# A GNN, attention and gated-cell layer on one core: the normalized input is no longer turned on TensorE, but loaded a second time already turned

## The chip, the core and the metric

The kernel runs on one core of a Trainium2 chip, as one program. The metric is the time of one execution in microseconds on the device; the median of three runs is given. Engines are named as in the profile: PE (TensorE), DVE (VectorE), ACT (ScalarE), POOL (GpSimd), SP (SyncE, which issues most transfers).

## What is computed

N = 1250 rows of D = 1024 numbers, 40000 edges of 8 types. Cut to what matters:

```
xn = layernorm(x)                                    # per row: (x - mean) / sqrt(var + eps)
u  = xn @ root + bias + sum_r mean_r(xn over edges) @ weight[r]
z  = concat(u, xn) @ w_gate + b_gate
h  = tanh(u) * z + xn * (1 - z)
q, k = elu(xn @ Wq) + 1, elu(xn @ Wk) + 1;  v = xn @ Wv;  g = sigmoid(xn @ Wg + bg)
kv = per head k.T @ v;  attention = (q * SCALE) @ kv / (q @ k_sum) * g @ Wo
x1 = x + h + attention
out = x1 + sigmoid(..) * tanh(sigmoid(..) * tanh(..))   # three products of layernorm(x1)
```

## The kernel before

**Products.** Rows are taken in T = 10 tiles of 128 (the last has 98). The work is a list of units, `UNIT`, numbered q: one stage (a weight half of 512 columns) times one tile. Stages run in the order Y (8 relation weights, two halves each), R, V, K, V, K, X, G, Q, O, C, then I, T, F twice. A unit is K = 8 steps k, and each step is three matmuls, since every operand is held as a high part (fp32r) and a low part (the rest): high by high, high by low, low by high. `aThi` and `aTlo` hold the turned activations, `Whi` and `Wlo` the weights. A unit's sums go to one of three banks of `acc` (q % 3) and leave it on ACT (Y and V, `evict`, L982) or DVE.

**How the order is set.** Each engine's instructions are written out by hand, with semaphores. All engines walk the same list of units and steps; work beside the products is hung on a unit and a step by tables. For the input x these are `LN_AT` (in which unit tile t is normalized on DVE, `ln_x`) and `TURN_AT` (in which unit tile t is turned). The first twelve units take the two halves of relation 0 tile by tile, so tile 1 is first needed in unit 2, tile 2 in unit 4, tile 3 in unit 6, tile 4 in unit 8, tile 5 in unit 10, tiles 6 to 9 in units 12 to 15.

**Input path.** For tile t: SP loads `xr` (a ring of XS = 4 tiles); DVE takes mean and variance (`bn_stats`, `bn_aggr`), ACT the root, DVE refines it in four tiny operations and writes `xnb` (L1143); PE turns it in eight 128x128 transposes into `tp` (`turn_x`, L815); ACT casts them to `aThi` (L974), DVE takes the rest into `aTlo` (L1121), and PE may start the tile (`x_lo`). POOL adds `xr` and `xnb` (`rows_sum`, L1620), and SP stores both (`x_rows`); `next_x(t)` waits until the sum of tile t is stored and loads tile t + XS into its place.

**Weights.** `hi_w` casts a granule of 128x1024 to `Whi` on ACT (L970), `lo_w` takes the rest on DVE (L1116); granules 2, 3, 5 and 7 of the first eight are done on POOL (`POOL_LO`, L1696).

**Later.** In stage K, `exponent` (ACT: relu L993, exp L995) and `elu_high` (DVE, L1399) make elu + 1 in `res`, and `kv_tile` (PE, L850) adds k.T @ v per pair of heads six steps into the next unit. In stage Q (24 units of 384 or 482 columns, `Wq` stationary, L955) the same chain ends in `read_out` (PE, L864) five steps into the next unit. The sums of R, X, G and of the last stages leave PSUM with a bias added, on DVE (L1420).

Of the kernel before, what the change touches and what calls it, by code (L numbers as in the profile page):

```python
# [14 lines left out]
N = 1250  # L15
D = 1024
# [33 lines left out]
XS = 4  # L50
# [3 lines left out]
U_SEMS, TH_SEMS = 6, 4  # L54
POOL_LO = (2, 3, 5, 7)
# [52 lines left out]
KIND = [STAGE[s][0] for s, _ in UNIT]  # L108
BY_ACT_TO = [sum(k in BY_ACT for k in KIND[:q + 1]) for q in range(UNITS)]
# [4 lines left out]
LN_AT = {0: 2, 2: 3, 4: 4, 6: 5, 7: 6, 8: 7, 9: 8, 10: 9}  # L114
TURN_AT = {1: 1, 3: 2, 5: 3, 7: 4, 8: 5, 9: 6, 10: 7, 11: 8, 12: 9}
# [81 lines left out]
def build(nc, x, src, dst, edge_type, weight, root, bias, w_gate, b_gate, Wq, Wk, Wv, Wg, bg, Wo,  # L197
          W_iT, b_i, W_oT, b_o, W_cT, b_c, out):
    with ExitStack() as ctx:
# [19 lines left out]
        code_d = dram("code_d", [RUN_ROWS, RUN])  # L219
        sample_d = dram("sample_d", [SAMPLES])  # L220
# [24 lines left out]
        stats = put("stats", [128, 16])  # L245
        x1_stats = put("x1_stats", [128, T, 12])
# [19 lines left out]
        xnb = at(M + 16384, "xnb", [128, XS, D])  # L266
        e_at = M + 32768
# [20 lines left out]
        most = at(M + 45248, "most", [128, T])
        assert M + 45312 <= end and M + 41024 + up(16 * COLS) + 32 * T <= M + 44512
# [44 lines left out]
        assert M + 49472 <= end  # L334
# [15 lines left out]
        def turned_rows(w):  # L350
# [4 lines left out]
        w_hi, w_lo, w_lo_pool, prod = sem("w_hi"), sem("w_lo"), sem("w_lo_pool"), sem("prod")  # L355
# [7 lines left out]
        ln_var, ln_root, ln_done, xs_made, x_turned, x_hi, x_lo = (  # L363
            sem(n) for n in ("ln_var", "ln_root", "ln_done", "xs_made", "x_turned", "x_hi", "x_lo"))
# [52 lines left out]
        def wait_w_lo(engine, n):  # L417

            if n in POOL_LO:
# [1384 lines left out]
```

## Time and profile before

| | before |
|---|---|
| median of 3 runs | 2206.23 us (2205.47 to 2206.28) |
| the profiled execution: time / span | 2205.51 us / 2203.7 us |
| PE busy | 2185.2 us, 99% of the span |
| DVE, ACT, POOL busy | 1176.2, 439.2, 737.6 us |
| granted PE clock, mean | 0.998 |

The span runs from the first to the last instruction; the time of the execution lies 1.8 us above it. A busy share is that of the whole span; matmuls overlap, so it says that PE had always one in flight, not that it ran at its peak.

### The profile page before, as it was taken

The numbers are of one execution on the slowest core, as the hardware profiler recorded it, in microseconds if no ns is written. First come the engines' busy times: TensorE is split into PE (matmuls) and PEld (weight loads), VectorE is DVE, ScalarE is ACT, GpSimd is POOL, SyncE is SP. The second block draws the span as 40 slices with busy tenths as digits, with TensorE's granted clock in tenths as the row PEclk, the third lists the DMA queues.
The fourth block names the chain that finished last, engine by engine and source line by source line (L and its number), as shares of the span: only waits on it lengthen the run. The fifth ranks groups of instructions, "written<-read, shape, count | busy, mean of one in ns | idle before, by whom it ended". The sixth has DMA issues, their size and how long they took to land.

```text
span 2203.7 us, 25068 instructions
## 1 busy us (share of the span) xinstructions
PE 2185.2 (99%) x9858; PEld 1776.6 (81%) x9858; DVE 1176.2 (53%) x1606; ACT 439.2 (20%) x617; POOL 737.6 (33%) x601
## 2 busy tenths in 40 slices
PE   7999999999999999999999999999999999999998
PEld 6878888888888888888888888889988888888887
DVE  5322678726666666676665676653432367234233
ACT  3221111211111111100221200112321314121121
POOL 5203002055555555544645354621210453000000
PEclk9999999999999999999999999999999999999999
DMA  7543321457788988784969788853126885103102
GB/s 251 183 131 97 109 85 48 134 183 220 261 293 281 312 301 306 242 271 141 318 223 318 238 292 299 274 177 134 49 77 225 274 285 170 39 29 125 59 30 79
DMA packets 191153, 416.59 MB, mean 189 GB/s; under 512 B 33938, under 2 KB 44563, under 8 KB 191035
## 3 DMA queue, kind: packets, MB, share of 16 engines
q1 hardware_dynamic: 127834, 229.10, 30.8%
q0 software_dynamic: 63200, 185.89, 25.4%
q8 instruction: 77, 1.26, 0.2%
q14 instruction: 42, 0.34, 0.0%
HBM read 352.34 MB, written 103.66 MB: 207 GB/s over the span
## 4 chain that ended last, share of the span: by engine, by line
PE 99%; DVE 1%; DMA 0%; ACT 0%; SPq 0%; issue 0%; DVEq 0%; ACTq 0%
PE acc L960 91%; PE acc L955 5%; PE tp L815 2%; PE agg L864 1%; PE tp L850 0%; PE misc L850 0%; DMA Wraw<-in_L_gnn_weight 0%; DVE Wlo L1116 0%; DVE stats L1135 0%; PE misc L864 0%; DVE aTlo L1519 0%; ACT L995 0%; DVE stats L1128 0%; ACT Whi L970 0%; SPq L515 0%
## 5 line engine op out<-in xcount | busy, mean ns | idle before, releaser
L960 PE MATMUL acc<-Whi,aThi 128*128 128x512 f32 (+1 forms) x2880 | 1141.2, 396 | 3.9 <-DVE aTlo L1519 2.1
L960 PE MATMUL acc<-Whi,aTlo 128*128 128x512 f32 (+1 forms) x2880 | 1135.4, 394 | 0.0
L960 PE MATMUL acc<-Wlo,aThi 128*128 128x512 f32 (+1 forms) x2880 | 1131.9, 393 | 0.0
L960 PEld LDWEIGHTS acc<-Whi,aTlo 128*128 128x128 f32 (+1 forms) x2880 | 534.1, 185 | 134.0
L960 PEld LDWEIGHTS acc<-Whi,aThi 128*128 128x128 f32 (+1 forms) x2880 | 534.2, 186 | 133.6 <-DVE aTlo L1519 2.5
L960 PEld LDWEIGHTS acc<-Wlo,aThi 128*128 128x128 f32 (+1 forms) x2880 | 535.3, 186 | 131.5
L1657 POOL DMA_INDIRECT ring<-y_d,edge x390 | 488.0, 1251 | 424.9 <-DVE U L1312 154.4
L1116 DVE TENSOR_TENSOR Wlo<-Wraw,Whi 128x1024 fp32r<-128x1024 f32 x148 | 185.5, 1255 | 314.6 <-ACT Whi L970 313.8
L982 ACT COPY res<-acc 128x512 f32<-128x512 f32 (+1 forms) x180 | 105.7, 587 | 837.7 <-PE acc L960 823.4
L1312 DVE SCALAR_TENSOR_TENSOR U<-ring,edge,U 128x1024 f32<-128x1024 f32 x180 | 230.2, 1279 | 24.2 <-DMA ring<-y_d,edge 24.0
L1312 DVE SCALAR_TENSOR_TENSOR odd<-ring,edge,odd 128x1024 f32<-128x1024 f32 x170 | 217.4, 1279 | 24.6 <-DMA ring<-y_d,edge 24.3
L970 ACT CAST Whi<-Wraw 128x1024 fp32r<-128x1024 f32 x152 | 158.9, 1047 | 199.6 <-DMA Wraw<-in_L_gnn_w_gate 71.9
L1420 DVE TENSOR_TENSOR res<-acc,bias_sb 128x512 f32<-128x512 f32 x100 | 69.2, 692 | 217.9 <-PE acc L960 128.5
L1644 POOL DMA_INDIRECT slot_d<-table,slot x20 | 21.8, 1088 | 227.9 <-DVEq L1272 222.4
L1028 ACT ACTIVATE res<-res 128x512 f32<-128x512 f32 (+1 forms) x60 | 38.0, 633 | 286.0 <-DVE res L1420 286.0
L1399 DVE SCALAR_TENSOR_TENSOR res<-acc,res 128x512 f32<-128x512 f32 (+3 forms) x44 | 28.0, 637 | 105.9 <-ACT res L995 105.9
L1121 DVE TENSOR_TENSOR aTlo<-tp,aThi 128x1024 fp32r<-128x1024 f32 (+1 forms) x39 | 46.7, 1197 | 59.9 <-ACT aThi L974 59.9
L1767 POOL TENSOR_TENSOR og<-og,part 128x384 f32<-128x384 f32 (+1 forms) x32 | 27.7, 875 | 128.2 <-DVE part L1452 128.2
L955 PE MATMUL acc<-aThi,Whi 128*128 128x384 f32 (+1 forms) x192 | 69.9, 364 | 0.0
L955 PE MATMUL acc<-aThi,Wlo 128*128 128x384 f32 (+1 forms) x192 | 67.6, 352 | 0.0
L955 PE MATMUL acc<-aTlo,Whi 128*128 128x384 f32 (+1 forms) x192 | 67.5, 352 | 0.0
L993 ACT ACTIVATE res<-acc 128x512 f32<-128x512 f32 (+3 forms) x44 | 24.4, 555 | 183.0 <-PE acc L960 94.5
(165 smaller groups left out, 1053.1 us busy)
## 6 DMA issues: line engine op xcount, KB each, us to landing
y_d<-res SPq DMA_DIRECT2D x144, 256.0 KB
Wraw<-in_L_gnn_weight SPq DMA_DIRECT2D x64, 512.0 KB, 5.6
Wraw<-in_L_gnn_w_gate SPq DMA_DIRECT2D x16, 512.0 KB, 6.7
ring<-y_d,edge POOLq DMA_INDIRECT x390, 6.3
xr<-in_x SPq DMA_DIRECT2D x9, 512.0 KB, 4.3
xn_d<-xnb SPq DMA_DIRECT2D x9, 512.0 KB, 5.4
xs_d<-xr SPq DMA_DIRECT2D x9, 512.0 KB, 5.8
ur_d<-res SPq DMA_DIRECT2D x18, 256.0 KB
```

Source lines behind the costliest of these rows:

```text
L815: tr = nc.tensor.transpose(tp[:, k // 4, (k % 4) * 128:(k % 4) * 128 + w], parts(k), ident[0:w, 0:w])
L955: mm = nc.tensor.matmul(to, a[:, s % 2, k, cols], b[:, k, c0:c0 + w], start=start, stop=stop)
L960: mm = nc.tensor.matmul(to, a[:, k, rows(i)], b[:, s % 2, k, :], start=start, stop=stop)
L970: nc.scalar.copy(granule(Whi, n), granule(Wraw, n)).then_inc(w_hi, 1)
L982: nc.scalar.copy(res[0:width(i), q % 3, :], acc[0:width(i), q % 3, :]).then_inc(evac_a, 1)
L1028: nc.scalar.activation(a, a, ACT.Tanh if kind == T_ else ACT.Sigmoid).then_inc(gate_act, 1)
L1116: nc.vector.tensor_tensor(granule(Wlo, n), granule(Wraw, n), granule(Whi, n).bitcast(F32), ALU.subtract).then_inc(w_lo, 1)
L1121: nc.vector.tensor_tensor(aTlo[:, :, rows(t)], turned_rows(width(t)), aThi[:, :, rows(t)].bitcast(F32), ALU.subtract).then_inc(done, 1)
L1312: nc.vector.scalar_tensor_tensor(to, g, scale, to, ALU.mult, ALU.add).then_inc(u_acc, 1)
L1399: nc.vector.scalar_tensor_tensor(a, p, 0.0, a, ALU.max, ALU.add).then_inc(evac_v, 1)
L1420: nc.vector.tensor_tensor(to, p, bias_sb[0:w, n % 2, :], ALU.add).then_inc(evac_v, 1)
L1657: pool.indirect_dma_start(ring[:, j % RING, :], None, a, bass.IndirectOffsetOnAxis(ap=index, axis=0), bounds_check=top - 1, oob_is_err=Fal ...
```

## The change

- **Turned input.** The host passes x a second time, turned (`x_t`). SP loads tile t of it into `xt` (`load_xt`). A DVE operation subtracts the row's mean there (`mid_x`); the mean of each row, which now runs along the free dimension, is spread over the partitions by one matmul of ones with a diagonal of means (`spread_mean`, the diagonal `mean_on` made by ACT in `root_x`). ACT casts it to `aThi` (`hi_x`), DVE takes the rest (`lo_x`). The eight transposes of each tile are gone.
- **Inverse deviation later.** What is in `aThi` and `aTlo` is only centred. `rs` holds each row's inverse deviation and its negative. It is multiplied in where sums leave PSUM: as the scale of ACT's copies (Y, V) and of the relu of K, in a `scalar_tensor_tensor` in place of the add (R, X, G), in an extra DVE operation for K, and for Q, whose rows lie along the free dimension, in an extra DVE operation `scale_q` before the relu, with `rs_row` loaded from DRAM.
- **Rings and places.** XS is 3, not 4, so x of tile 3 is no longer among the first loads. `LN_AT` and `TURN_AT` change: tile 2 is normalized in unit 1, not 0; tiles 4 to 9 are centred one unit earlier.
- **First low parts.** All eight first granules are done by `lo_w` on DVE; POOL starts its row sums when they are done.
- **kv.** `kv_tile` does one matmul per head (64 stationary columns, 65 moving), the two heads of a pair to partitions 0 to 63 and 64 to 127, instead of one per pair (128 and 130).
- **Last unit.** Its columns are done in two halves, each evicted, gated and stored by itself.

```diff
-XS = 4
+XS = 3
-POOL_LO = (2, 3, 5, 7)
-LN_AT = {0: 2, 2: 3, 4: 4, 6: 5, 7: 6, 8: 7, 9: 8, 10: 9}
-TURN_AT = {1: 1, 3: 2, 5: 3, 7: 4, 8: 5, 9: 6, 10: 7, 11: 8, 12: 9}
+LN_AT = {1: 2, 2: 3, 4: 4, 6: 5, 7: 6, 8: 7, 9: 8, 10: 9}
+TURN_AT = {1: 1, 3: 2, 5: 3, 6: 4, 7: 5, 8: 6, 9: 7, 10: 8, 11: 9}
...
             load_x(0)
-            for n in range(4):
+            load_w(0)
+            load_xt(0)
+            for n in range(1, 4):
                 load_w(n)
             load_x(1)
             load_w(4)
             load_w(5)
-            load_x(2)
+            load_xt(1)
             load_w(6)
             load_w(7)
-            load_x(3)
+            load_x(2)
+            load_xt(2)
...
                 sp.wait_ge(xs_st[t % XS], 16 * (t // XS + 1))
                 load_x(t + XS)
+                load_xt(t + XS)
...
+            def spread_mean(t):
+                pe.wait_ge(mean_root, 2 * t + 1)
+                if t:
+                    pe.wait_ge(x_mid, with_halves(t - 1))
+                w = width(t)
+                nc.tensor.matmul(tp[:, 0, 0:w], ones_all[0:w, :], mean_on[0:w, t % 2, 0:w], start=True, stop=True
+                                 ).then_inc(mean_mm, 1)
...
                 for m in range(4):
-                    to = (misc[:, :] if m < 2 else tp[:, 0, :])[:, m % 2 * 130:m % 2 * 130 + 130]
-                    mm = nc.tensor.matmul(to, rows_k[:, m * 128:(m + 1) * 128], vld[0:w, t % 2, m, :],
-                                          start=(t == 0 and m % 2 == 0), stop=(t == T - 1), skip_group_check=True)
+                    for e in range(2):
+                        head = (2 * m + e) * HEAD
+                        mm = nc.tensor.matmul(misc[e * HEAD:(e + 1) * HEAD, m * 65:m * 65 + 65], rows_k[:, head:head + HEAD],
+                                              vld[0:w, t % 2, m, e * 65:e * 65 + 65], start=(t == 0 and m == 0),
+                                              stop=(t == T - 1), skip_group_check=True)
...
+                nc.scalar.activation(mean_on[0:w, t % 2, 0:w], ident[0:w, 0:w], ACT.Copy, scale=stats[0:w, 12:13]
+                                     ).then_inc(mean_root, 1)
+                act.wait_ge(ln_stats, 2 * t + 2)
+                nc.scalar.activation(stats[0:w, 15:16], stats[0:w, 14:15], ACT.Sqrt).then_inc(mean_root, 1)
...
+            def mid_x(t, part):
+                dve.wait_ge(xt_in[t % XS], 16 * (t // XS + 1))
+                dve.wait_ge(mean_mm, t + 1)
+                a, w = xt[:, t % XS, part, 0:width(t)], width(t)
+                mean = tp[:, 0, 0:w].unsqueeze(1).to_broadcast([128, part.stop - part.start, w])
+                nc.vector.tensor_tensor(a, a, mean, ALU.subtract).then_inc(x_mid, 1)
+            def lo_x(t, part, count):
+                dve.wait_ge(x_hi, count)
+                nc.vector.tensor_tensor(aTlo[:, part, rows(t)], xt[:, t % XS, part, 0:width(t)],
+                                        aThi[:, part, rows(t)].bitcast(F32), ALU.subtract).then_inc(x_lo, 1)
...
+            def scale_q(q):
+                i, h, n = UNIT[q][1], STAGE[UNIT[q][0]][2], 3 * STAGE[UNIT[q][0]][2] + UNIT[q][1] // 4
+                w = GROUPS[i // 4][1]
+                dve.wait_ge(prod, q + 1)
+                dve.wait_ge(rs_in[n % 2], 16 * (n // 2 + 1))
+                p = acc[:, q % 3, 0:w]
+                nc.vector.tensor_tensor(p, p, rs_row[:, n % 2, 0:w], ALU.mult).then_inc(q_scaled, 1)
...
-            for n in POOL_LO:
-                pool.wait_ge(w_hi, n + 1)
-                nc.gpsimd.tensor_tensor(granule(Wlo, n), granule(Wraw, n), granule(Whi, n).bitcast(F32),
-                                        ALU.subtract).then_inc(w_lo_pool, 1)
+            pool.wait_ge(w_lo, 2 * GRAN)
             rows_sum(0)
```

**SP, after the first loads.** The names: `xn_d` and `xs_d` are the stores of tile t's normalized rows and sums, `xr<-in_x` a load of a further tile. Before, the load waits for the store of tile 0 alone and stands ahead of tile 1's two stores:

```order
L720 DMA xn_d<-xnb 128x1024 [waits ln_done]
L722 DMA xs_d<-xr 128x1024 [waits xs_made]
L519 DMA xr<-in_x 128x1024 [waits xs_st0]
L720 DMA xn_d<-xnb 128x1024 [waits ln_done]
L722 DMA xs_d<-xr 128x1024 [waits xs_made]
L552 DMA y_d<-res 128x512 [waits evac_a]
```

That load is tile 4. In the changed kernel the first such load is tile 3:

```order
L743 DMA xn_d<-xnb 128x1024 [waits ln_done]
L745 DMA xs_d<-xr 128x1024 [waits xs_made]
L743 DMA xn_d<-xnb 128x1024 [waits ln_done]
L745 DMA xs_d<-xr 128x1024 [waits xs_made]
L528 DMA xr<-in_x 128x1024 [waits xs_st0]
L533 DMA xt<-in_x_t 128x8x128 [waits x_lo]
L572 DMA y_d<-res 128x512 [waits evac_a]
```

It has moved behind the store of tile 1's sums, and so behind POOL's second row sum.

**DVE, units 2 and 3.** Before, the low part of the tile turned in unit 3 (L1121) comes between the statistics of tile 3 (`x_in3`) and those of tile 4 (`x_in0`):

```order
L1128 BN_STATS stats<-xr 128x6 [waits x_in3]
L1128 BN_STATS stats<-xr 128x6
...
L1143 TENSOR_SCALAR xnb<-xr,stats 128x1024 [waits dve_step]
L1121 TENSOR_TENSOR aTlo<-tp,aThi 128x8x128 [waits x_hi]
L1128 BN_STATS stats<-xr 128x6 [waits x_in0]
```

Changed, tile 3's statistics wait for the ring's place 0 (`x_in0`), and the centring (L1234) and low part (L1239) of tile 2 follow them:

```order
L1207 BN_STATS stats<-xr 128x6 [waits x_in0]
L1207 BN_STATS stats<-xr 128x6
...
L1225 TENSOR_SCALAR xnb<-xr,stats,rs 128x1024 [waits xs_made,xn_st0]
L1234 TENSOR_TENSOR xt<-xt,tp 128x1024 [waits mean_mm,xt_in2]
L1239 TENSOR_TENSOR aTlo<-xt,aThi 128x8x128 [waits x_hi]
```

One instruction has been added ahead of the low part, and what they stand behind waits for a later load.

**POOL, from the first row sum.** In the changed kernel:

```order
L1754 TENSOR_TENSOR xr<-xr,xnb 128x1024 [waits ln_done,w_lo]
L1832 MEMSET caps 128x1 x10
...
L1759 CAST code<-raw_edges 125x320 [waits edges_in]
...
L1846 IOTA next_places 128x128
L1754 TENSOR_TENSOR xr<-xr,xnb 128x1024 [waits ln_done] x8
```

Before it stood the same way, with four `Wlo` granules ahead of it in place of the wait for `w_lo`: the edge codes lie between the first row sum and the second in both.

## Rows read from the trace of the kernel before

**Rows 1.** The page: busy us (share of the span) x instructions.

```profile
PE 2185.2 (99%) x9858; PEld 1776.6 (81%) x9858; DVE 1176.2 (53%) x1606; ACT 439.2 (20%) x617; POOL 737.6 (33%) x601
```

**Rows 2.** Groups on PE by shape: xcount | busy us, mean ns | idle before.

```profile
L850 PE MATMUL tp<-vld,res 128*128 128x130 f32 x72 | 11.0, 274 | 0.0
```

**Rows 3.** The chain that ended last: start us, us, what.

```profile
23.16 1.71 PE tp L815 x8
...
86.31 0.87 PE tp L815 x8
92.75 0.68 PE tp L815 x8
...
1091.38 0.45 PE tp L850 x4
...
2198.10 0.70 DVE res L1420
...
2200.22 0.69 DVE res L1513
```

**Rows 4.** Timeline of the start, all engines: start us, us, engine, line [idle before].

```profile
0.74 1.28 ACT L1054 ACT_TABLE_LOAD   x1 [0.74 <-PEq L1791]
...
5.64 0.21 DVE L1130 BATCH_NORM_AGGREGATE stats<-stats 128x2 f32<-128x12 f32 x1
...
11.76 2.40 DVE L1116 TENSOR_TENSOR Wlo<-Wraw,Whi 128x1024 fp32r<-128x1024 f32 x1
...
11.90 0.79 PE L960 MATMUL acc<-Whi,aThi 128*128 128x512 f32 x1 [2.12 <-DVE aTlo L1519]
...
15.48 0.47 PE L960 MATMUL acc<-Whi,aTlo 128*128 128x512 f32 x1
...
21.23 0.50 PE L960 MATMUL acc<-Whi,aThi 128*128 128x512 f32 x1 [1.82 <-DVE Wlo L1116]
```

**Rows 5.** Timeline of POOL from 20 us.

```profile
23.38 3.37 POOL L1620 TENSOR_TENSOR xr<-xr,xnb 128x1024 f32<-128x1024 f32 x1
26.69 0.40 POOL L1700 MEMSET caps<- 128x1 f32 x10
...
35.35 7.11 POOL L1620 TENSOR_TENSOR xr<-xr,xnb 128x1024 f32<-128x1024 f32 x3
```

**Rows 6.** Line 519, the loads of x: issue to landing.

```profile
DMA to landing us min/median/max: 3.5/4.3/12.2
```

**Rows 7.** Timeline of ACT: ends of units 1, 3, 12 and 13.

```profile
29.61 0.59 ACT L982 COPY res<-acc 128x512 f32<-128x512 f32 x1 [1.84 <-PE acc L960]
...
41.66 0.59 ACT L982 COPY res<-acc 128x512 f32<-128x512 f32 x1 [3.22 <-PE acc L960]
...
97.73 0.59 ACT L982 COPY res<-acc 128x512 f32<-128x512 f32 x1 [3.45 <-PE acc L960]
103.29 0.59 ACT L982 COPY res<-acc 128x512 f32<-128x512 f32 x1 [4.97 <-PE acc L960]
```

**Rows 8.** Timeline of DVE: one tile's statistics, normalization and low part.

```profile
63.62 1.27 DVE L1128 BATCH_NORM_STATS2 stats<-xr 128x6 f32<-128x512 f32 x2
...
66.39 0.16 DVE L1134 RECIPROCAL stats<-stats 128x1 f32<-128x1 f32 x1 [1.06 <-ACT stats L1054]
...
67.22 0.81 DVE L1143 TENSOR_SCALAR xnb<-xr,stats 128x1024 f32<-128x1024 f32 x1
68.93 1.22 DVE L1121 TENSOR_TENSOR aTlo<-tp,aThi 128x1024 fp32r<-128x1024 f32 x1 [0.89 <-ACT aThi L974]
```

**Rows 9.** Timeline after the second Q unit, all engines.

```profile
1499.55 0.56 DVE L1399 SCALAR_TENSOR_TENSOR res<-acc,res 128x384 f32<-128x384 f32 x1 [1.82 <-ACT res L995]
...
1500.60 0.81 PEld L864 LDWEIGHTS agg<-kv,res 128*128 128x128 f32 x6
```

**Rows 10.** Timelines of DVE and PE after the first K unit.

```profile
1089.52 0.69 DVE L1399 SCALAR_TENSOR_TENSOR res<-acc,res 128x512 f32<-128x512 f32 x1 [6.47 <-ACT res L995]
1090.78 0.61 PE L850 MATMUL misc<-vld,res 128*128 128x130 f32 x4
```

More of the change, by code:

```diff
@@ L194, in wait, with build @@
         engine.wait_ge(self.sem, self.n)
-def build(nc, x, src, dst, edge_type, weight, root, bias, w_gate, b_gate, Wq, Wk, Wv, Wg, bg, Wo,
+def build(nc, x, x_t, src, dst, edge_type, weight, root, bias, w_gate, b_gate, Wq, Wk, Wv, Wg, bg, Wo,
           W_iT, b_i, W_oT, b_o, W_cT, b_c, out):
@@ L415, in granule @@
             return a[:, s % 2, 2 * g:2 * g + 2, :]
-        def wait_w_lo(engine, n):
-            if n in POOL_LO:
-                engine.wait_ge(w_lo_pool, POOL_LO.index(n) + 1)
-            else:
-                engine.wait_ge(w_lo, n + 1 - sum(m < n for m in POOL_LO))
         def load_beside(q):
@@ L727, in next_x, with store_rs, load_rs @@
                 load_x(t + XS)
+                load_xt(t + XS)
+            def store_rs():
+                sp.wait_ge(ln_done, T)
+                for t in range(T):
+                    sp.dma_start(rs_d[rows(t)].rearrange("(p o) -> p o", o=1), rs[0:width(t), 0, t:t + 1]
+                                 ).then_inc(rs_st, 16)
+            def load_rs(h, g):
+                n = 3 * h + g
+                c0, w = GROUPS[g]
+                if n >= 2:
+                    wait_evicted(sp, place(Q_, (n - 2) // 3, 4 * ((n - 2) % 3) + 3))
+                sp.dma_start(rs_row[:, n % 2, 0:w], rs_d[c0:c0 + w].rearrange("(o n) -> o n", o=1)
+                             .to_broadcast([128, w])).then_inc(rs_in[n % 2], 16)
             x_rows(0)
@@ L960, in _ @@
                             mm = nc.tensor.matmul(to, a[:, k, rows(i)], b[:, s % 2, k, :], start=start, stop=stop)
-                mm.then_inc(prod, 1)
+                if q != FINAL:
+                    mm.then_inc(prod, 1)
+                    continue
+                for e, c in enumerate(FINAL_PARTS):
+                    for k in range(K):
+                        for a, b, start, stop in ((aThi, Whi, k == 0, False), (aThi, Wlo, False, False),
+                                                  (aTlo, Whi, False, k == K - 1)):
+                            mm = nc.tensor.matmul(final_sums(e), a[:, k, rows(i)], b[:, s % 2, k, c], start=start,
+                                                  stop=stop)
+                    mm.then_inc(prod, 1)
         @block.scalar
@@ L981, in evict @@
                 act.wait_ge(prod, q + 1)
[L982 removed]
+                if s < 2:
+                    act.wait_ge(ln_done, i + 1)
+                nc.scalar.activation(res[0:width(i), q % 3, :], acc[0:width(i), q % 3, :], ACT.Copy,
+                                     scale=rs[0:width(i), 0, i:i + 1]).then_inc(evac_a, 1)
             def exponent(q):
@@ L1028, in gate_function, with final_gate @@
                 nc.scalar.activation(a, a, ACT.Tanh if kind == T_ else ACT.Sigmoid).then_inc(gate_act, 1)
+            def final_gate():
+                for e, c in enumerate(FINAL_PARTS):
+                    act.wait_ge(evac_v, BY_DVE_TO[FINAL] + e)
+                    a = res[0:width(T - 1), FINAL % 3, c]
+                    nc.scalar.activation(a, a, ACT.Sigmoid).then_inc(gate_act, 1)
             def cell_tanh(q):
@@ L1538, in _ @@
                             make_x1(q - 1)
+                        if kind == Q_:
+                            scale_q(q - 1)
                     if q and k == 2:
```

247 lines of the change are left out of this document (152 added, 95 removed).

## The prediction

> **What bounds the kernel now.** I read the page first: PE is busy for 99% of the span, so only what lengthens or shortens PE's own stream counts, and any other engine counts where PE waits for it [rows 1]. Then I read the groups on PE by shape and the chain that ended last, for what PE does beside the products: the transposes of x take 1.71 us once and then 0.87 us a tile (0.68 us for the last of 98 rows), nine of them inside the units, and a `kv_tile` takes 2 x 0.45 us, in eight instructions [rows 2, 3]. Then the timelines: of the start, where PE begins its first product at 11.90 us and waits 1.82 us once more, at 21.23 us, for a low part of a weight [rows 4]; of ACT, whose copies mark where units end: unit 1 at 29.61, unit 3 at 41.66, unit 12 at 97.73, unit 13 at 103.29, so that a unit with nothing beside it is 5.56 us [rows 7]. From there on PE's stream has no hole but at the first Q unit, so a change at the start passes to the end in full.
>
> **The start, up to the end of unit 1.** The statistics of tile 0 are there at 5.85 us [rows 4]. ACT now makes the diagonal first, which needs a table other than the root's, and its load stands behind the wait for the statistics; before, the only load ran at 0.74 us under the wait for x [rows 4]. That puts 1.28 us on the path: 7.1 us; the diagonal some 0.3 us, the mean's matmul at the low clock some 0.7 us: 8.2 us. Two centring halves (0.69 us each is what the halves took before, about half of the 1.22 us of [rows 8]) end near 9.7; the small operations 1.0, the normalization 0.81 [rows 8], the first weight granule and the first low half 1.8 us: PE starts near 13.6 us, 1.7 us later. DVE then has all eight granules and tile 1's statistics (some 4 us), at 1.2 us a granule, and is through at about 26.1 us. Before, POOL did four, but a DVE granule beside it took 2.40 us [rows 4]; that is given back, so unit 1 ends near 30.4 us and not 29.61. **+0.8 us**, between -1 (POOL's absence pays for more) and +3 (the third transfer, in pieces of 512 B, delays every weight behind it).
>
> **Units 2 and 3.** Two units of 5.56 and one mean matmul instead of a turn of 0.87 us. A mean is a 128-column matmul in two instructions; by the transposes, one instruction each, 0.109 us [rows 3], it is 0.22 us. **-0.65 us.** PE could begin unit 4 at 41.4 us.
>
> **The hole before unit 4.** This is the term that decides. With XS = 3, x of tile 3 is not among the first loads. By the order, SP issues it only behind the store of tile 1's sums, which waits for POOL's second `rows_sum`; between POOL's first and second stand the edge codes. POOL starts the first when the eighth low part is done, 26.1 us; a row sum undisturbed is 7.11 / 3 = 2.4 us: 28.5. From `caps` to the second sum POOL took 35.35 - 26.69 = 8.66 us [rows 5], less 0.2 for the memset that is moved ahead: 37.0; the second sum: 39.4. Store and load are issued by 39.8, and a load of x lands after 4.3 us, 3.5 at best [rows 6]: 44.1. DVE has stood in `ln_x(3)` since 34 us, and tile 2's centring and low part, which PE needs for unit 4, are queued behind it. From the landing: statistics to normalized rows took 67.22 + 0.81 - 63.62 = 4.4 us with 1.06 us of waiting for ACT [rows 8]; with ACT free, a diagonal and one more small operation it is 3.9: 48.0. Centring 1.2, ACT's cast 1.05, low part 1.2, three hops between engines: 51.6. PE waits from 41.4 to 51.6: **+10.2 us**. Bounds: 7 if POOL starts 2 us sooner and the load lands in 3.5; 13 if the sums take the 3.37 us of [rows 5] and the load 6.
>
> After it PE is cold: the first product's eight matmuls took 15.48 - 11.90 = 3.58 us at the lower level, where eight at the higher take 8 x 5.56 / 24 = 1.85 [rows 4, 7]. **+1.7 us**, 0 to 3.
>
> **Units 4 to 12.** Before, 97.73 - 41.66 = 56.07 us [rows 7]: nine units and seven turns, 6.0 us. Now seven means, 1.5 us: **-4.5 us**. But in units 6 to 10 DVE has a tile's statistics (3.9), another's centring (1.2), the wait for the cast (1.1) and the low part (1.2): 7.4 us for a PE unit of 5.78. PE's mean matmul of tile t waits for the centring of tile t - 1. In unit 8 there are 0.9 us to spare, in unit 9 it is 0.7 late, in 10 and 11 1.65 each: **+4.0 us**, 0 to 6.
>
> The new low part reads two SBUF tiles, where the old read PSUM. Beside a POOL operation such an instruction took 2.40 us instead of about 1.2 [rows 4]. POOL's sum starts with the end of the normalization and lasts 2.4 us, the low part is due 2.3 us after it: 0.1 us, in the bounds. The Trainium skill (SBUF — State Buffer, "Who interferes with whom") says so as a rule: a DVE instruction with two SBUF inputs is shut out while a GpSimd instruction that reads SBUF runs. By that rule every low part could meet a sum and wait up to 2.4 us; the row agrees on the mechanism, and the order of the two decides that little is lost.
>
> **kv.** Twenty tiles, 0.90 us each. The moving columns are the same in total (16 x 65 for 8 x 130), so at the same rate it stays 0.90. No row shows matmuls on half of the columns. If both halves ran at once, 0.45 us: -9 us. If each of 16 instructions took what the smallest on record took, 0.68 / 8 = 0.085 us [rows 3], 1.36 us: +9 us. I take near the same rate, **+1 us**. The Trainium skill (TensorEngine Tiling (Array Packing), "Key Properties") says that tiles run in parallel, which would give the -9, and that a change of tiling mode drains the engine, which pushes the other way twice a tile. No row of this trace decides between them. The extra DVE operation fits: the first K unit's single one ended at 1090.21 and kv's first matmul began at 1090.78 [rows 10], its weights being loaded some 0.3 us earlier, so 0.7 us more is 0.4 us late, once; the others have 1.8 us.
>
> **Q.** In a 384-column unit the relu waits for `scale_q`, 0.56 us and a hop, 0.6. The high part was done at 1500.11, and PE loads it as weights at 1500.60 [rows 9]: 0.46 us of cover, so 0.14 us late in each of 16 units, 2.2; 0.6 in the first, where PE waits already; 0.3 where a turned tile holds DVE. **+3.1 us**, 0 to 6.
>
> **The end.** Four operations, 2198.10 to 2200.91 [rows 3]. In halves, of the second half remain its add, then two each of multiply and add at about 0.4: 2.0 us. **-1.0 us**, with a smaller store. V, R, X, G: the scale sits in instructions that were there; nothing, PE being 5 us per unit ahead of need.
>
> **Sum.** 0.8 - 0.65 + 10.2 + 1.7 - 4.5 + 4.0 + 1.4 + 3.1 - 1.0 = +15.0 us on the profiled 2205.5 us: 2220.5. That execution lies 0.7 us below the median shown, within the spread of a microsecond; I say 2220.
>
> **Rivals.** *A, 0.58:* the above, 2214 to 2227. *B, 0.14, the column halves overlap:* PE would do a kv in about half; the separate partitions speak for it, two instructions per head, each pair on one half, against. 15 - 10 = +5: 2211. *C, 0.18, the hole does not form:* if x of tile 3 lands before about 33 us DVE is never held. That needs SP's load ahead of POOL's second sum; the order speaks against it, and my reading of what DVE and SP wait for could be wrong in one count. Then 10.2, 1.7 and the DVE lag 4.0 are gone: -0.9, 2204.6, not slower; it decides from a landing after 34 us, beyond which each us costs PE one. *D, 0.10, kv pays per instruction:* +9, 2228.
>
> **Range and chances.** 0.2% is 4.4 us, about what a measurement tells from no change. Faster than 2201.8: the part of C in which kv or Q also come out well, 0.12. Same (2201.8 to 2210.6): the rest of C and the lower part of B, 0.13. Slower: A, D and the rest, 0.75. The 8 in 10 reach from 2205, inside C, to 2231, above D; A alone, 2214 to 2227.
>
> **What would show it.** Right: PE idle for about 10 us before the first product of unit 4, released by DVE's low part; DVE idle before the statistics of tile 3 until the load lands; that load issued after POOL's second sum; PE waits of 1 to 2 us before mean matmuls in units 9 to 11; 0.1 us before each read-out in Q; kv near 0.9 us. Wrong: x of tile 3 issued before 30 us, or PE's stream unbroken to unit 13, or kv tiles of 0.5 us, each of which takes its own term away.

## The result and the profile after

The changed kernel takes 2218.4 us (2217.62 to 2219.55, 6 runs), the kernel before 2206.15 beside it (2205.47 to 2207.42): a ratio of 1.0056, 95% interval 1.0044 to 1.0068. The profiled execution took 2217.98 us, its span 2215.7 against 2203.7 before. So it is 12 us slower; forecast were 2220 and slower.

The page of the changed kernel, to be held against [rows 1]:

```profile
PE 2180.6 (98%) x9982; PEld 1762.3 (80%) x9982; DVE 1220.4 (55%) x1669; ACT 462.8 (21%) x629; POOL 716.5 (32%) x597
```

PE is busy for 4.6 us less than before in a span that is 12 us longer: the work beside the products did get smaller, and the time went into waits. Its own view of waits says for whom (us in total, times, longest):

```profile
PE acc L1005 <- DVE aTlo L1239: 16.2, 3, 10.4
PE tp L871 <- ACT mean_on L1124: 8.0, 1, 8.0
PE tp L871 <- DVE xt L1234: 2.8, 3, 1.3
PE agg L909 <- DVE res L1521: 1.7, 3, 1.2
PE acc L1005 <- DVE Wlo L1195: 1.4, 1, 1.4
PE misc L894 <- issue: 0.2, 1, 0.2
```

The timeline of PE has each of them in its place (start, duration, what, and in brackets the idle time before it):

```profile
13.55 0.80 PE L1005 MATMUL acc<-Whi,aThi 128*128 128x512 f32 x1 [4.81 <-DVE aTlo L1239]
22.41 0.50 PE L1005 MATMUL acc<-Whi,aThi 128*128 128x512 f32 x1 [1.38 <-DVE Wlo L1195]
29.38 0.50 PE L1005 MATMUL acc<-Whi,aThi 128*128 128x512 f32 x1 [0.94 <-DVE aTlo L1239]
51.45 0.76 PE L1005 MATMUL acc<-Whi,aThi 128*128 128x512 f32 x1 [10.45 <-DVE aTlo L1239]
...
83.65 0.46 PE L871 MATMUL tp<-mean_on,ones_all 128*128 128x128 f32 x2 [0.29 <-DVE xt L1234]
90.94 0.46 PE L871 MATMUL tp<-mean_on,ones_all 128*128 128x128 f32 x2 [1.27 <-DVE xt L1234]
98.18 0.43 PE L871 MATMUL tp<-mean_on,ones_all 98*128 98x98 f32 x2 [1.21 <-DVE xt L1234]
```

At 51.45 is the hole before unit 4, and the chain that ended last tells how it is made:

```profile
36.64 2.37 POOL xr L1754
39.03 0.32 SPq L745
39.35 0.04 issue
39.39 4.56 DMA xr<-in_x
43.95 0.02 issue
43.97 1.30 DVE stats L1207 x2
...
47.70 1.23 DVE xt L1234
48.95 1.06 ACT aThi L1131
50.03 1.28 DVE aTlo L1239
```

Read upwards from the low part: it is tile 2's, it waited for tile 2's cast and centring, and those stood on DVE behind the statistics of tile 3, whose x came with a load issued after POOL's second row sum.

To see where the 12 us arise I compared the same events in both traces. In the column "so far" is the start of the event after less the start before, in the last column what has been added since the row above.

| event | before, us | after, us | so far | gained there |
|---|---|---|---|---|
| copy of unit 12 (ACT) | 97.73 | 108.47 | +10.74 | +10.74 |
| first kv matmul | 1090.78 | 1101.93 | +11.15 | +0.41 |
| last kv tile | 1268.83 | 1278.48 | +9.65 | -1.50 |
| first Q unit | 1487.81 | 1497.28 | +9.47 | -0.18 |
| first read-out | 1495.81 | 1505.53 | +9.72 | +0.25 |
| read-out 21 of 24 | 1602.92 | 1615.40 | +12.48 | +2.76 |
| last matmul ends | 2198.02 | 2211.07 | +13.05 | +0.57 |
| end of the span | 2203.7 | 2215.7 | +12.0 | -1.05 |

### The profile page after: what moved, and what is told of

Same layout as the page of the kernel before. It is cut to its first block, busy times and chain, and to the rows that moved or that the text cites. A ratio compares the mean times of both kernels' runs of the same rounds, so it can differ in the third digit from the quotient of the medians.

```text
span 2215.7 us, 25455 instructions
## 1 busy us (share of the span) xinstructions
PE 2180.6 (98%) x9982; PEld 1762.3 (80%) x9982; DVE 1220.4 (55%) x1669; ACT 462.8 (21%) x629; POOL 716.5 (32%) x597
## 3 DMA queue, kind: packets, MB, share of 16 engines
q8 instruction: 78, 1.28, 0.2%
## 4 chain that ended last, share of the span: by engine, by line
PE 95%; DVE 2%; DMA 1%; ACT 1%; POOL 1%; issue 1%; SPq 0%; DVEq 0%; ACTq 0%; POOLq 0%
PE acc L1005 87%; PE acc L1000 4%; PE tp L862 1%; PE agg L909 1%; PE misc L894 1%; DMA Wraw<-in_L_mix_Wq 0%; DVE Wlo L1195 0%; DVE stats L1207 0%; DVE xt L1234 0%; DVE aTlo L1239 0%; DMA xr<-in_x 0%; ACT aThi L1131 0%; POOL xr L1754 0%; ACT mean_on L1124 0%; PE agg L1013 0%
## 5 line engine op out<-in xcount | busy, mean ns | idle before, releaser
L1791 POOL DMA_INDIRECT ring<-y_d,edge x390 | 479.9, 1231 | 432.2 <-DVE U L1408 161.3
L1038 ACT ACTIVATE res<-acc,rs 128x512 f32<-128x512 f32 (+1 forms) x180 | 124.1, 690 | 792.5 <-PE acc L1005 757.0
L1408 DVE SCALAR_TENSOR_TENSOR odd<-ring,edge,odd 128x1024 f32<-128x1024 f32 x170 | 217.6, 1280 | 28.9 <-DMA ring<-y_d,edge 28.5
L1552 DVE SCALAR_TENSOR_TENSOR res<-acc,rs,bias_sb 128x512 f32<-128x512 f32 (+1 forms) x60 | 45.1, 751 | 101.5 <-issue 80.4
L1555 DVE TENSOR_TENSOR res<-acc,bias_sb 128x512 f32<-128x512 f32 (+1 forms) x39 | 27.0, 692 | 109.7 <-PE acc L1005 94.9
L1903 POOL TENSOR_TENSOR uio<-uio,tx 128x1024 f32<-128x1024 f32 (+1 forms) x10 | 24.0, 2401 | 104.3 <-ACT uio L1061 96.0
L1200 DVE TENSOR_TENSOR aTlo<-tp,aThi 128x1024 fp32r<-128x1024 f32 (+1 forms) x30 | 35.9, 1197 | 31.8 <-ACT aThi L1028 31.8
```

The lines of the kernel that those rows point to most:

```text
L1038: nc.scalar.activation(res[0:width(i), q % 3, :], acc[0:width(i), q % 3, :], ACT.Copy, scale=rs[0:width(i), 0, i:i + 1]).then_inc(evac_a, 1)
L1200: nc.vector.tensor_tensor(aTlo[:, :, rows(t)], turned_rows(width(t)), aThi[:, :, rows(t)].bitcast(F32), ALU.subtract).then_inc(done, 1)
L1408: nc.vector.scalar_tensor_tensor(to, g, scale, to, ALU.mult, ALU.add).then_inc(u_acc, 1)
L1552: nc.vector.scalar_tensor_tensor(to, p, rs[0:w, 0, i:i + 1], bias_sb[0:w, n % 2, :], ALU.mult, ALU.add).then_inc(evac_v, 1)
L1555: nc.vector.tensor_tensor(to, p, bias_sb[0:w, n % 2, :], ALU.add).then_inc(evac_v, 1)
L1791: pool.indirect_dma_start(ring[:, j % RING, :], None, a, bass.IndirectOffsetOnAxis(ap=index, axis=0), bounds_check=top - 1, oob_is_err=Fal ...
```

## The experiments

All times below are medians; the kernel before, run beside them, had medians of 2205.6 to 2206.3. Line numbers of a variant can differ by a few from those of the change.

### 1. The load first

SyncE's loop, at each unit:

```
+ if q in LN_AT and 2 <= LN_AT[q] < T - XS + 2:
+     next_x(LN_AT[q] - 2)
  if q in TURN_AT:
      x_rows(TURN_AT[q])
- if q in LN_AT and 2 <= LN_AT[q] < T - XS + 2:
-     next_x(LN_AT[q] - 2)
```

> SyncE asks for the fourth tile's two loads before it waits for the second tile's row sum. Theory (the hole before unit 4 is the late x load, and the load is late because of SyncE's order): the load of tile 3 is issued at about 31.5 us instead of 39.39, VectorE's statistics of tile 3 start at about 36 instead of 43.97, unit 4 starts at about 43.5 instead of 51.45, PE's idle time before it falls from 10.45 to about 2.5 us; some 1 us comes back as longer waits of the mean matmuls (VectorE needs 7.3 us per tile against TensorE's 5.8). Time 2218.4 - 8 - 1 + 1, about 2210. Rival 1 (the load only seems late; VectorE is the bound whatever comes in): unit 4 still starts after 49 us, time within 2 us of 2218. Rival 2 (the time is given back in full further on, because VectorE is behind from unit 7 to unit 12 anyway): unit 4 at 43.5, but the waits of units 7 to 10 grow by 6 us or more, time over 2215.

Measured: 2217.61 us. Unit 4 began at 45.91 with 4.97 us of idle time, as the theory had it, and the time did not fall. On PE's timeline further on:

```profile
45.91 0.76 PE L1005 MATMUL acc<-Whi,aThi 128*128 128x512 f32 x1 [4.97 <-DVE aTlo L1239]
...
79.11 0.46 PE L871 MATMUL tp<-mean_on,ones_all 128*128 128x128 f32 x2 [0.58 <-DVE xt L1234]
89.34 0.77 PE L871 MATMUL tp<-mean_on,ones_all 128*128 128x128 f32 x2 [4.21 <-DVE xt L1234]
98.48 0.43 PE L871 MATMUL tp<-mean_on,ones_all 98*128 98x98 f32 x2 [0.49 <-DVE xt L1234]
```

and on DVE's, whose statistics now wait for x:

```profile
84.25 1.29 DVE L1207 BATCH_NORM_STATS2 stats<-xr 128x6 f32<-128x512 f32 x2 [2.87 <-DMA xr<-in_x]
```

The waits sum to 10.25 us instead of 13.22. The 3 us gained went into the clock: behind the wait at 89.34, twelve matmuls ran 0.43 us apart instead of 0.23, 2.4 us, and unit 4 had eleven such instead of seven, 0.8. (The second of these is scatter and not the edit's doing: behind the same hole of 10.4 us the stretch was 7 to 13 matmuls long in other runs, see the last section.) My edit had done more than it was meant to: for every tile, the store of a tile's rows now stood on SyncE behind the wait for the store of the tile before, so that from one x load to the next it took 9 to 10 us (61.23, 70.35, 80.62, 89.63) where DVE wants one every 7.3. Rival 2 was right in its numbers, and it stayed open whether it was right in its reason.

### 2. The load first, once

The same swap at unit 1 alone, for tile 3's loads:

```
+ if q == 1:
+     next_x(0)
  if q in TURN_AT:
      x_rows(TURN_AT[q])
- if q in LN_AT and 2 <= LN_AT[q] < T - XS + 2:
+ if q != 1 and q in LN_AT and 2 <= LN_AT[q] < T - XS + 2:
      next_x(LN_AT[q] - 2)
```

> As the first experiment, but SyncE's order is changed only for the fourth tile's loads; for later tiles the store of a tile's rows again stands ahead of the wait for the earlier store, as in the change. In the first experiment the hole before unit 4 fell from 10.45 to 4.97 us and the time did not: a wait of 4.21 us had come at 89.34, where VectorE waited 2.87 us for an x load that SyncE issued late. Theory (that give-back is the experiment's own side effect): unit 4 starts at 45.9 as there, VectorE goes on with a tile every 7.3 us from 55.6 instead of 60.5, the mean matmuls' waits stay near 2.8 us in sum, and the time falls by about 4.5 us, to 2213 or 2214. Rival (units 7 to 12 are bound by VectorE or the ring of three whatever happens before, so that any gain at unit 4 is given back there): waits of 7 us or more in units 7 to 10, time 2216 or more.

Measured: 2213.05 us (2212.13 to 2213.61), 5.35 less than the change. The hole was 4.96 us, 5.49 less than in the change:

```profile
46.02 0.57 PE L1007 MATMUL acc<-Whi,aThi 128*128 128x512 f32 x1 [4.96 <-DVE aTlo L1241]
```

The three waits behind it were 0.29, 1.27 and 1.21, to the hundredth those of the change. So the give-back of run 1 was the edit's own, and here the hole's length passes to the end nearly one to one.

### 3. Tile 3's statistics behind tile 2's low part

```
 # VectorE; ScalarE's root_x(3) likewise
+if q == 3 and k == 5:
+    ln_x(3)
-if k == (4 if q == 1 else 0) and q in LN_AT:
+if k == (4 if q == 1 else 0) and q in LN_AT and q != 2:
     ln_x(LN_AT[q])
```

> The statistics and scale of tile 3 are moved on VectorE (and its root on ScalarE) to behind tile 2's centring and low part; loads as in the change. Theory (the hole is a queue: tile 2's centring stands behind tile 3's statistics, which wait for a load): the load still lands at about 44 us, but unit 4 starts at about 41.5 with under 1 us of idle time, unit 6 waits up to 1 us, and the waits of the mean matmuls grow from 2.8 to about 4 us. Time about 2218.4 - 10 - 1.5 (no cold stretch behind the hole) + 1.7, so 2208 to 2209. Rival (what is late is tile 3 itself, and moving it back only moves the hole to unit 6): idle time of 8 us or more before unit 6, time 2216 or more.

Measured: 2214.32 us, 4.1 less than the change and 6 more than I expected. The hole before unit 4 is gone (1.59 us are left), so it was a queue and no lack of data for tile 2. But 1.40 us came before unit 6 and 3.16 before the mean beside unit 7, where the loads of x, as late as before, were now on the path; all waits sum to 8.9 us. What is left before unit 4 is this low part of DVE, with POOL's row sums beside it (timelines of the two engines):

```profile
39.25 3.18 DVE L1241 TENSOR_TENSOR aTlo<-xt,aThi 128x1024 fp32r<-128x1024 f32 x1 [1.12 <-ACT aThi L1131]
```
```profile
36.58 4.76 POOL L1758 TENSOR_TENSOR xr<-xr,xnb 128x1024 f32<-128x1024 f32 x2
```

It took 3.18 us instead of 1.3 and ended 1.1 us after POOL: it stood still while POOL summed.

### 4. Means further apart

With the edit of 3, and

```
-LN_AT = {1: 2, 2: 3, 4: 4, 6: 5, 7: 6, 8: 7, 9: 8, 10: 9}
-TURN_AT = {1: 1, 3: 2, 5: 3, 6: 4, 7: 5, 8: 6, 9: 7, 10: 8, 11: 9}
+LN_AT = {1: 2, 2: 3, 6: 4, 8: 5, 9: 6, 10: 7, 11: 8, 13: 9}
+TURN_AT = {1: 1, 3: 2, 5: 3, 7: 4, 8: 5, 9: 6, 10: 7, 12: 8, 13: 9}
 # SyncE, behind x_rows(TURN_AT[q])
-if q in LN_AT and 2 <= LN_AT[q] < T - XS + 2:
-    next_x(LN_AT[q] - 2)
+    if TURN_AT[q] - 1 + XS < T:
+        next_x(TURN_AT[q] - 1)
```

> Tile 3's statistics behind tile 2's low part, as in the second experiment, and the centrings of tiles 4 to 9 set further apart (beside units 7, 8, 9, 10, 12 and 13 instead of 6 to 11, statistics likewise), each next load right behind the store of the tile before. The second experiment still had waits of 1.59, 1.40, 3.16, 0.30, 1.27 and 1.22 us, 8.9 us in sum. Theory (from unit 6 on TensorE waits only because mean matmuls stand in its queue before they are needed: VectorE needs 7.3 us a tile, TensorE 5.8 us a unit, but tiles 6 to 9 are first used in units 12 to 15): the wait of about 1.6 us before unit 4 stays, the sum of all others falls under 2 us, time 2214.3 - 5, about 2209. Rival (VectorE or the loads are late for the products themselves): waits move to units 8 to 15 and their sum stays over 7 us, time 2213 or more.

Measured: 2207.16 us (2206.95 to 2207.47), ratio to before 1.0005 (0.9996 to 1.0015): the whole loss is gone but for what can't be told from nothing. The waits left are 1.59 us before unit 4 and

```profile
74.25 0.49 PE L871 MATMUL tp<-mean_on,ones_all 128*128 128x128 f32 x2 [1.25 <-ACT mean_on L1124]
81.56 0.49 PE L871 MATMUL tp<-mean_on,ones_all 128*128 128x128 f32 x2 [1.26 <-ACT mean_on L1124]
```

So neither DVE nor the ring of three was too slow for the products; the mean matmuls stood too early in PE's queue. The edit moved the loads too, each to right behind the store of the tile before: in run 3 DVE waited up to 2.7 us for x between 44 and 70 us, here only once, 1.6 us. How much of the gain is the loads' and how much the means' was not measured apart, and a ring of four with the changed kernel was not tried.

### 5. The form of kv: before's, halves apart, half the work

Three runs for one term. The first takes back `kv_tile`, `kv_to_sbuf` and the layout of `vld`:

> The change with the K^T V block as before the change: four matmuls of 128x130 per tile into two banks. Read from the two traces a tile's block and the lengthening of the 24 matmuls behind it cost 0.90 us before and 0.62 + 0.21 = 0.83 after. Theory (the eight half matmuls cost about as many columns as the four whole ones, and save 0.07 us per tile): 20 tiles, +1.4 us, and the 0.25 us stall ahead of the first tile goes or stays: time 2219.5 to 2220. Rival 1 (halves run beside each other, and something else in the K stages hides it): 9 us slower than the change, 2227. Rival 2 (halves pay a change of mode at each block that the 0.21 us shows): up to 4 us faster than the change, 2214.

The second only swaps the two loops of `kv_tile`, `for e in range(2)` outside `for m in range(4)`:

> The change with the eight half matmuls of a K^T V tile in another order: the four on columns 0 to 63, then the four on columns 64 to 127. Theory (neighbouring halves do not overlap; a matmul of 65 columns takes half of one of 130): the block keeps its 0.62 us and a tile of the K stages its period of 6.37 us, time as the change. Rival (alternating halves overlap in part, or loads of one half hide behind the other's stream): the block grows by 0.1 us or more, period over 6.45, 2 us or more over 20 tiles.

The third has `for m in range(2 if t else 4)`:

> The change with half of the K^T V products left out (of every tile but the first of each half, only the first four of the eight half matmuls are made, so the output is wrong there). It splits a tile's 0.83 us into a part per matmul and a part per block. Theory (0.62 us are eight matmuls in alternating halves, 0.21 us is paid once per block, where weight loads wait 0.36 us): the block takes 0.31 us and the 24 matmuls behind it still 5.76 us, a period of 6.07 us. Rival (all of the 0.83 us goes by the number of matmuls): 24 matmuls take 5.65 us, a period of 5.96 us.

Measured: 2221.0 us for before's form, 2.6 over the change (1.6 of it between the first and the last kv tile), 2223.62 (one run) for halves apart and 2214.65 (one run) for half the work. What lies outside the kv tiles is scatter: the first kv matmul already came 0.7 to 1.0 us later than in the change, in before's form because twelve matmuls and not seven ran at the lower clock behind the hole before unit 4. From the first kv tile to the last it is 176.55 us in the change, 178.15, 181.87 and 172.55 in the three runs. The chain in the K stages, of the change, of halves apart, and of half the work:

```profile
1108.38 0.61 PE misc L894 x16
1108.99 5.76 PE acc L1005 x24
1114.75 0.62 PE misc L894 x16
```
```profile
1109.33 0.90 PE misc L894 x16
1110.23 5.75 PE acc L1005 x24
1115.98 0.90 PE misc L894 x16
```
```profile
1109.17 0.38 PE misc L894 x8
1109.56 5.76 PE acc L1005 x24
1115.31 0.38 PE misc L894 x8
```

Before's form has 0.90 for kv and 5.55 for the products, a period of 6.45 us; the change 6.37; halves apart 6.65. My theory of "the same rate, no overlap" fell with the second run: the same eight matmuls take 0.62 us when the column halves alternate and 0.90 when they do not, so neighbours on different halves do run partly beside each other. From the third, four matmuls fewer save 0.24 us; if the cost is linear in their number, eight are then 0.48, about half of the 0.90, and 0.62 - 0.48 = 0.14 in the block and 0.21 in the products behind it are paid per block whatever is in it. PE's weight loads show the place: 0.36 us of idle time ahead of each block. The Trainium skill (TensorEngine Tiling (Array Packing), "Key Properties") has both halves of this, that tiles run in parallel and that a change of tiling mode drains the engine; here they come to -0.42 and +0.35 us a tile, and nearly cancel. That the fixed 0.35 us is that drain is a reading with the page's help, not shown here.

### 6. Q without its scale

`scale_q` keeps its waits on VectorE and does nothing, and ScalarE's relu no longer waits for it.

> The change without the multiplication of the Q sums by the row of inverse deviations (its waits on VectorE stay; ScalarE's relu no longer waits for VectorE). The output then has an unscaled Q. Theory (read-outs come late because the relu waits for a VectorE operation of 0.57 to 0.68 us): read-outs stand 4.88 us apart again instead of 5.06 in the narrow groups, from the first read-out to the thirteenth or so 2.8 us are saved, the first read-out's wait falls from 1.24 to about 0.7 us; time 3 us under the change, 2215.3. Rival (the Q stage's loss is that of the three queues' extra loads of the row, or of the fewer columns free in PSUM): read-outs stay 5.06 us apart, time as the change.

Measured: 2214.18 us in one run, its span 3.5 us shorter than the change's. The read-out matmuls by shape, of the change and of this run (count, busy us, mean ns, idle):

```profile
L909 PE MATMUL agg<-kv,res 128*128 128x130 f32 x144 | 21.0, 282 | 1.7 <-DVE res L1521 1.7
```
```profile
L909 PE MATMUL agg<-kv,res 128*128 128x130 f32 x144 | 20.0, 275 | 0.6 <-DVE res L1520 0.6
```

From the first read-out to number 21 it is 107.05 us, in the change 109.87, before 107.11. Of the loss in this stretch, 2.8 us, the scale's wait is the whole. Ahead of it, the first read-out comes 7.66 us behind the first Q matmul, in the change 8.25, before 8.00: the scale costs 0.59 us there too, and the change has gained 0.34 us by something else that was not traced.

### 7. The end in one piece

The last unit again whole, as before the change.

> The change with the last unit in one piece, as before the change. Theory (by the two traces the halves cost 0.09 us more on TensorE and take 1.05 us off what comes behind the last matmul): from the last matmul to the end of the span 5.7 us instead of 4.63, and the last unit 0.1 us shorter: time 1.0 us over the change, 2219.4. Rival (the halves only look shorter, the second store then lands at the same time): the tail stays within 0.3 us of 4.63.

Measured: 2218.52 us in one run. Its last matmul ended at 2210.76 and its span at 2216.6: a tail of 5.84 us against 4.63. The halves save 1.2 us there and cost 0.09 on PE; the median of the change can't tell that from nothing, the tail can.

### 8. The table early

```
+act.wait_ge(const, 1)
+nc.scalar.activation(warm[:, :], ones_all[:, 0:1], ACT.Sqrt)
 act.wait_ge(const, 3)
 root_x(0)
```

> The change with only the early square root on ScalarE (its table is loaded before the first statistics come, at 0.7 us or so instead of 7.85, and the load at 6.13 falls away if the copy with a scale is in the same table). Theory (the first mean waits for table loads: 1.28 us ahead of the diagonal, and 1.28 us more ahead of the first weight copy): the first mean matmul starts at about 6.7 us instead of 7.97, unit 0 at about 12.3 instead of 13.55, unit 2 at 28.2 instead of 29.38, and as GpSimd's first sum also comes 1.2 us earlier, unit 4 at 50.3 instead of 51.45: time 1.2 us less, 2217.2. Rival 1 (the scaled copy takes its own table whatever was loaded): nothing moves but the second load; time under 0.3 us less. Rival 2 (from unit 0 on VectorE's eight low parts and the weights' landings bound the start): unit 0 earlier, unit 2 and all behind it not; time as the change.

Measured: 2218.01 us, ratio 1.0053 as the change's 1.0056. Both table loads (the change has one at 6.13 for the diagonal and one at 7.85 for the root, 1.28 us each) left the path: there is one at 0.74 us and none after it, so the diagonal and the root do with the same table once the root comes first. The first mean matmul began at 6.64, and unit 0 at 13.26, 0.3 us sooner, not 1.3. DVE's timeline says why:

```profile
8.56 1.29 DVE L1237 TENSOR_TENSOR xt<-xt,tp 128x512 f32<-128x512 f32 x2 [2.38 <-DMA xt<-in_x_t]
```

The centring needs the turned input, and that lands at 8.5 us. My theory and rival 1 both left that out; rival 2 is nearest, with the landing of another load than the one it named. In the profiled execution even the 0.3 was lost again further on: thirteen matmuls ran at the lower clock behind the hole before unit 4, and not seven. The medians, 0.4 us apart, can't tell a gain of 0.3 from nothing.

### 9. The front mended, and the turned input first

All of it together: load first once (2), tile 3's statistics behind (3), the table early (8), `TURN_AT = {1: 1, 3: 2, 5: 3, 7: 4, 8: 5, 9: 6, 11: 7, 12: 8, 14: 9}` with statistics to suit and the later loads placed as in run 4, and on POOL

```
 rows_sum(0)
+pool.wait_ge(x_lo, with_halves(1))
+rows_sum(1)
+rows_sum(2)
 ...
 edge_codes()
 ...
-rows_sum(1)
-for t in range(2, T):
+for t in range(3, T):
```

> Everything that the runs so far pointed to: tile 3's loads asked for once ahead of the store of tile 1's rows, tile 3's statistics behind tile 2's low part, the centrings of tiles 4 to 9 beside units 7, 8, 9, 11, 12 and 14, GpSimd's row sums of tiles 1 and 2 ahead of the edge codes (the first of them only behind tile 1's low part), and an early square root of a constant on ScalarE, so that its table is loaded before the first statistics come. From the 2207.2 of the sixth experiment: the start 1.2 us earlier (one table load of 1.28 off its path), the low part of tile 2 back from 3.18 to 1.3 us, because GpSimd's row sum no longer runs beside it (1.6 us of TensorE wait), one wait of 1.25 us for a mean instead of two. Sum 4.0: 2203.2, under the kernel before by 0.1%. Rival 1 (the early table gives nothing, since the first weights or VectorE hold the start): 2204.5. Rival 2 (GpSimd's sums, put earlier, lengthen VectorE's work on tile 2 or the fifth unit's loads and cost what they save): 2206 or more.

Measured: 2203.9 us (2203.44 to 2204.97), ratio 0.9991 (0.9982 to 1.0000). No wait before unit 4, one of 1.24 us at 72.25; the low part that had taken 3.18 us now has no row sum beside it:

```profile
39.04 1.38 DVE L1246 TENSOR_TENSOR aTlo<-xt,aThi 128x1024 fp32r<-128x1024 f32 x1 [1.12 <-ACT aThi L1134]
```

Run 8 pointed to one more edit, `load_xt(0)` ahead of `load_w(0)`:

> The mended version (ninth run) with the first tile's turned input asked for ahead of the first weight granule. In the ninth and tenth runs VectorE waited 2.23 and 2.38 us for that load until 8.6 us, although the mean was there at 7.4, so the early table gave only 0.2 to 0.3 us; and from 8.6 to 29 us VectorE had hardly a gap. Theory (that landing holds the whole start): the load lands some 1 us earlier, the first centring starts at 7.5 to 7.8, unit 0 at 12.3 instead of 13.31, unit 2 at 28.2 instead of 29.15, and the time falls by 0.9 us, from 2203.9 to 2203.0. Rival (the first weight granule, now 1 us later, is then what VectorE waits for, at 11.4 us): unit 0 at 13.3 or later and no gain, 2203.9 or up to 0.5 us more.

Measured: 2202.66 us (2202.35 to 2203.38), ratio 0.9984 (0.9975 to 0.9993). The centring starts at 7.55 and waits for the mean now, not for a load, unit 0 starts at 12.40, unit 2 at 28.25, each 0.9 us sooner:

```profile
7.55 1.29 DVE L1241 TENSOR_TENSOR xt<-xt,tp 128x512 f32<-128x512 f32 x2 [1.34 <-PE tp L874]
```

This version beats both kernels: 3.6 us under the one before, 15.7 under the change.

## Why the prediction was right, step by step

**The hole before unit 4** (forecast +10.2, PE starting at 51.6): 10.45 us, starting at 51.45. Each link stood within 0.4 us: first sum done at 28.25 (28.5), load issued at 39.39 (39.8), statistics at 43.97 (44.1), centring at 47.70 (48.0). Runs 2 and 3 took away either cause, the late load or the queue, and the hole went from 10.45 to 4.96 and 1.59 us; this is shown. Rival C is thereby settled for this kernel: the hole does form. Its price for a kernel without it, 2204.6, is near what runs 4 and 9 reached, 2207.2 and 2203.9, but partly by luck: it contains a kv term that was 2.5 us too high, and run 4 still has 4.1 us of waits.

**Cold behind it** (+1.7): seven matmuls 0.43 us apart instead of 0.23, until 54.57, and a slow first one; the copy of unit 4 came 7.4 us after its first product, 1.75 more than a unit takes. In run 4, with 1.59 us of idle time before it, unit 4 starts at the full clock, and this is gone too. That the term was met to 0.05 us is luck: other runs with the same hole have up to thirteen such matmuls, 1.2 us more.

**The start** (+0.8): the mechanism was wrong, the first number right by chance. PE did start at 13.55 (13.6), but run 8 shows that the table, on which I had put 1.28 us, costs 0.3; the rest was the landing of the turned input, which I had not priced. The step in between was nearly right too, the eight low parts done at 25.76 us and not 26.1, but unit 2 began at 29.38, where I had unit 1 end at 30.4, and before it began at 29.41: the term is nil and not +0.8. What I left out is unit 1 of the kernel before. From its first matmul to unit 2 it took 8.18 us, since the turn of tile 1 in it took 1.71 us and from 22.5 to 26 us the granted clock (third column from the end) was at the lower level; in the change it is 6.97 us, 0.94 us of waiting for tile 1's low part included.

```profile
22.50:24.50 2.00, 2.00 (x10) 1.77 (x9) 2.00 (x2) 0.00 (x0) 2.00 (x2) 0.50 0.33 116
24.50:26.00 1.50, 1.50 (x6) 1.24 (x5) 1.43 (x5) 0.00 (x0) 1.50 (x1) 0.55 0.25 98
```

PE was ready for unit 4 at 41.00 and not 41.4; up to there the change had gained 0.55 us by the copies' time (41.66 in [rows 7], some 0.1 behind the product), where my two terms have a loss of 0.15. The 41.4 does not even follow from these two terms, which give 41.7 from that row: 0.3 us of the hole was counted twice in the sum.

**Units 4 to 12** (-4.5, and +4.0 for DVE behind): the waits came in units 9, 10 and 11 as said, but were 0.29, 1.27 and 1.21 us and not 0.7, 1.65 and 1.65; a tile takes DVE 7.30 us and not 7.4, and PE's unit with a mean 5.81 and not 5.78. The idle times alone are 2.8 us; but the mean matmuls of units 9 to 11 lie 6.25, 7.29 and 7.24 us behind the one before instead of 5.81, so the term is 3.35 instead of 4.0. The means cost 0.25 us each and not 0.22: -4.3. By unit 12: -0.55 + 10.45 + 1.75 - 4.3 + 3.35 = +10.7, measured +10.74; my terms had come to +11.55.

**kv** (+1): the sign was wrong, by way of a wrong picture. The sum per tile hardly moved (0.90 to 0.83 us, -1.5 in all), but not since the rate stays: overlap and a fixed cost per block nearly cancel (run 5). Rivals B and D each had one half of it, and as outcomes both are wrong. This is the term that was most mis-sized, 2.5 us. The first K unit's +0.4 was +0.41, if what lies between unit 12 and the first kv matmul is all its doing.

**Q** (+3.1): +0.25 for the first read-out, where I said 0.6, and +2.76 for the rest, where I said 2.5. Run 6 shows that the scale's wait is the cause: it costs 0.59 at the first read-out, as I said, less 0.34 of a gain that is not explained, and 2.8 behind it. In the narrow groups the read-outs stand 5.06 us apart and not 4.88, 0.18 us late each and not 0.14; in the wide ones (6.16 us apart both times) nothing is lost.

**The end** (-1.0): -1.05 in the trace; run 7, one execution, has 1.2.

Not forecast: +0.48 us of the 0.57 between the 21st read-out and the last unit. A low part of DVE at 1842.75 is on the chain of the change and not on that of before, which is some 0.3; the rest is not placed, and this stays open.

The sum was 3 us too high for the profiled execution (15.0 against 12.0): kv 2.5, the start 0.7 and DVE 0.65 too high, the hole 0.25 and the means 0.2 too low, and 0.57 not forecast. Against that, 0.18 us gained between the last kv tile and the first Q unit is in no term either.

## What to carry to other kernels

Here the smaller ring cost nothing that could be measured by its size (run 4 keeps it and is level with the kernel before) and 10 us by its order: look for the first tile that is no longer loaded ahead, follow who frees its slot through every queue (here GpSimd, SyncE, VectorE), and see what unrelated work stands behind the waiting instruction. A matmul that only prepares a later unit belongs in TensorE's queue no earlier than its input is surely there; setting six of them further apart, with the loads to suit, and moving one block of statistics gave back 11 of 12 us. And when an experiment removes a wait and the time stays, read the trace before believing that the gain is "given back": run 1 was its own edit's doing.

## What the runs showed of the hardware

**The waits of 3.16 us and more cost clock as well, those of 1.61 us and less did not.** Behind idle times of 10.45, 4.96, 4.21 and 3.16 us the granted clock fell to the lower of its levels, 1.2 GHz (matmuls 0.43 us apart instead of 0.23); behind 1.61, 1.59, 1.40 and 1.27 us it did not. In between there is one wait of 1.82 us, in the kernel before at 21.23 us: PE went on at the full clock, and from 22.5 to 26 us the clock was low. How long the low stretch lasts differs from execution to execution of nearly the same wait: behind the hole of 10.4 to 10.6 us it was 7 matmuls in the change and run 7, 9 in run 6, 10 and 12 in run 5, 13 in run 8, up to 1.2 us of difference. So a difference of 1 us between single executions with such a hole says little. In two stretches of run 1, right behind its waits of 4.97 and 4.21 us, the granted clock is the third column from the end:

```profile
46.00:52.00 6.00, 6.00 (x17) 4.71 (x18) 3.24 (x10) 0.49 (x2) 1.89 (x1) 0.61 0.84 305
...
89.00:96.00 7.00, 6.66 (x19) 5.36 (x20) 3.59 (x9) 2.10 (x4) 1.51 (x1) 0.56 0.75 219
```

**What stands still beside a GpSimd sum.** In run 1 DVE did its small operations on tile 3's statistics while POOL summed rows (36.55 to 41.30):

```profile
37.57 1.40 DVE L1218 SCALAR_TENSOR_TENSOR stats<-stats 128x1 f32<-128x1 f32 x1
39.00 0.15 DVE L1219 TENSOR_SCALAR stats<-stats 128x1 f32<-128x1 f32 x1
39.19 2.12 DVE L1220 TENSOR_TENSOR rs<-stats 128x1 f32<-128x1 f32 x1
41.35 0.15 DVE L1221 TENSOR_SCALAR rs<-rs 128x1 f32<-128x1 f32 x1
```

The two with two SBUF inputs, 0.22 and 0.16 us elsewhere, took 1.40 and 2.12 and ended at 38.97 and 41.31, about the ends of the two sums; those with one input took their usual 0.15. The Trainium skill (SBUF — State Buffer, "Who interferes with whom") has it so: a DVE instruction with two SBUF inputs contends with a GpSimd instruction that reads SBUF, one with a single input, outside the modes in which VectorE takes both ports, does not. The trace agrees, 2.12 us against 0.15. In the prediction I had priced this at 0.1 us, which holds for the change, where DVE stood idle in that stretch: the price appears only once the hole is mended, which is why the mend in run 9 moves POOL's sums too.

**Alternating column halves.** 0.62 us for eight half matmuls in alternation, 0.90 in two runs of four. Some 0.35 us of the change's 0.83 a tile is paid per block, whatever is in it: 0.14 inside the 0.62 and 0.21 in the products behind (run 5).
